# Last pair of expert slots: up product in two column halves, down product with the contraction outermost, one-hot products at the end

## The reference

```python
logits = t @ switch_w + switch_b
route_prob = jax.nn.softmax(logits, axis=-1)
route_prob_max = jnp.max(route_prob, axis=-1)
routes = jnp.argmax(route_prob, axis=-1)
for e in range(n_experts):
    h = jax.nn.gelu(t @ w1[e] + b1[e])      # 1024 -> 512
    y = h @ w2[e] + b2[e]                   # 512 -> 1024
    out = jnp.where((routes == e)[:, None], y, out)
out = out * route_prob_max[:, None]
```

## Time and profile before

| | us |
|---|---|
| median of 3 runs | 586.93 (584.77 to 587.86) |
| profiled execution | 584.88 |
| its span, first to last instruction | 583.2 |
| TensorE matmul busy | 554.5 (95%) |
| VectorE busy | 381.9 (65%) |
| ScalarE busy | 240.0 (41%) |
| up product of the last pair begins | 552.92 |
| last row add on VectorE ends | 578.20 |

### The profile page before, as it was taken

The page is one execution under the profiler, slowest core; times in us unless marked ns, Lnnn a source line. Parts: engine busy times, 40 slices in busy tenths (PEclk is TensorE's granted clock), DMA queues, the critical chain, the costliest instruction groups (busy, mean ns, idle before and its releaser), DMA issues.

```text
span 583.2 us, 8532 instructions
## 1 busy us (share of the span) xinstructions
PE 554.5 (95%) x3054; PEld 473.9 (81%) x3054; DVE 381.9 (65%) x747; ACT 240.0 (41%) x390; POOL 148.4 (25%) x161
## 2 busy tenths in 40 slices
PE   3989999999999999999999999999998998999985
PEld 3989997897999999999979999999997886633321
DVE  6688887865777346773548888888889886200114
ACT  3646554320243333353427556756576513320000
POOL 5627666851176500081000001001002010000020
PEclk9999999999999999999999999999998997999999
DMA  8655557530263554438523125416349688199943
GB/s 304 215 141 184 176 167 248 143 112 1 63 180 128 170 196 137 142 119 287 162 82 132 58 90 123 128 58 160 132 156 326 225 311 338 62 383 412 411 174 112
DMA packets 33778, 104.19 MB, mean 179 GB/s; under 512 B 5424, under 2 KB 9712, under 8 KB 33744
## 3 DMA queue, kind: packets, MB, share of 16 engines
q1 hardware_dynamic: 28224, 89.95, 44.6%
q0 software_dynamic: 5376, 13.29, 8.6%
q10 hardware_dynamic: 144, 0.52, 0.3%
HBM read 96.58 MB, written 5.60 MB: 175 GB/s over the span
## 4 chain that ended last, share of the span: by engine, by line
PE 80%; DVE 11%; ACT 4%; issue 3%; DMA 1%; POOL 0%; DVEq 0%; SPq 0%; ACTq 0%
PE ps L1604 41%; PE ps L1955 10%; PE ps L1797 6%; PE ps L1618 5%; DVE wsp L954 4%; PE ps L1901 2%; PE ps L1741 2%; PE ps L1751 2%; PE ps L1726 2%; PE ps L1688 2%; PE ps L1669 2%; PE ps L1761 2%; ACT wsp L660 1%; DMA tok<-in_x 1%; DVE big L954 1%
## 5 line engine op out<-in xcount | busy, mean ns | idle before, releaser
L1604 PE MATMUL ps<-big,wsp 128*128 128x384 f32 x1656 | 295.7, 336 | 3.2 <-DVE wsp L954 2.7
L1604 PEld LDWEIGHTS ps<-big,wsp 128*128 128x128 f32 x1656 | 286.0, 188 | 7.8 <-issue 5.3
L954 DVE TENSOR_TENSOR wsp<-raw,wsp 128x1024 fp32r<-128x1024 f32 x85 | 110.5, 1304 | 30.4 <-ACT wsp L660 29.5
L660 ACT ACTIVATE wsp<-raw 128x1024 fp32r<-128x1024 f32 x83 | 86.9, 1052 | 32.9 <-PE ps L1618 12.9
L569 POOL DMA_INDIRECT edge_table<-ef,eidx x48 | 56.0, 1167 | 33.0 <-DMA edge_table<-ef,eidx 19.2
L667 ACT ACTIVATE big<-ps,bias 128x384 f32 x24 | 14.0, 583 | 80.8 <-PE ps L1604 80.8
L1955 PE MATMUL ps<-blocks 128*64 128x512 f32 x192 | 43.8, 599 | 0.0
L965 DVE SCALAR_TENSOR_TENSOR big<-ps,bias,big 128x384 f32 (+1 forms) x24 | 14.8, 617 | 34.2 <-ACT big L667 33.5
L784 ACT ACTIVATE work<-work,snm 128x384 f32<-128x384 f32 x48 | 28.9, 604 | 16.1 <-DVE snm L1221 16.1
L1618 PE MATMUL ps<-wsp,big 128*128 128x512 f32 x144 | 33.2, 390 | 0.3 <-DVE wsp L954 0.3
L1618 PEld LDWEIGHTS ps<-wsp,big 128*128 128x128 f32 x144 | 26.9, 188 | 6.3 <-DVE wsp L954 0.8
(11 more groups left out here) (249 smaller groups left out, 715.3 us busy)
## 6 DMA issues: line engine op xcount, KB each, us to landing
raw<-in_w_stream SPq DMA_DIRECT2D x85, 512.0 KB, 4.1
blocks<-in_w_experts SPq DMA_DIRECT2D x64, 512.0 KB, 9.1
rowbuf<-in_rowb POOLq DMA_DIRECT2D x6, 512.0 KB, 6.6
raw_x<-in_w_stream SPq DMA_DIRECT2D x4, 512.0 KB, 6.3
slot_y<-rowbuf POOLq DMA_DIRECT2D x7, 256.0 KB, 5.7
tok<-in_x SPq DMA_DIRECT2D x3, 512.0 KB, 4.0
edges_a<-in_src_rows SPq DMA_DIRECT2D x8, 192.0 KB
edges_a<-in_dst_rows SPq DMA_DIRECT2D x8, 192.0 KB
```

The lines of the kernel that those rows point to most:

```text
L660: nc.scalar.activation(wsp[:, 0, slot, :], raw[:, slot, :], ACT.Copy).then_inc(w_hi, 1)
L954: return nc.vector.tensor_tensor(dst, value, hi.bitcast(F32), ALU.subtract)
L1604: ins = nc.tensor.matmul(ps[:, bank, 0:N], wsp[:, a, slot, k * P:(k + 1) * P], moving[:, b, k, :], start=(k == 0 and n == 0), stop=(k == K ...
```

## The change

Three edits, all in the last pair. (a) The up product is computed as columns 0 to 255 for all eight contraction steps, then columns 256 to 511, each half in its own PSUM bank with its own bias product; all eight blocks are waited for at the start. ScalarE's copy and Gelu and TensorE's transposes work on halves, and the transposes of half 0 stand in the middle of the second half of the up product, those of half 1 behind the first quarter of the down product. (b) The down product first does contraction steps 0 and 1 for both halves of the columns, then steps 2 and 3 for both; both bias products stand ahead. The blocks are loaded in that order. (c) Both groups of one-hot products stand at the end, and VectorE copies y half 0 after the first two gathered row adds and not ahead of them.

```diff
+DOWN_ORDER = ((0, 1, 2, 3),) * (TWOS - 1) + ((0, 2, 1, 3),)
 def down_blocks(p):
-    return [s * QE + RING + j for j in range(RING) for s in (2 * p, 2 * p + 1)]
+    return [s * QE + RING + j for j in DOWN_ORDER[p] for s in (2 * p, 2 * p + 1)]
...
+            def copy_up_half(half):
+                if half == 0:
+                    act.wait_ge(u_half, 1)
+                else:
+                    act.wait_ge(blk_read, read_after("up", TWOS - 1))
+                nc.scalar.activation(u_buf[:, half * 2 * P:(half + 1) * 2 * P], ps[:, 1 - half, 0:2 * P], ACT.Copy)\
+                    .then_inc(u_copied, 1)
+            def hidden_half(half):
+                act.wait_ge(ht_ready, TWOS + half)
+                nc.scalar.activation(h_buf[(TWOS - 1) % 2][:, half * 2 * P:(half + 1) * 2 * P],
+                                     ps[:, 2 + half, 0:2 * P], ACT.Gelu_apprx_tanh).then_inc(ht_act, 1)
...
-            for p in range(TWOS):
+            for p in range(TWOS - 1):
                 copy_up(p)
                 hidden(p)
+            for half in range(2):
+                copy_up_half(half)
+            for half in range(2):
+                hidden_half(half)
...
-                dve.wait_ge(blk_read, read_after("down", p, 2 * h + 2))
+                dve.wait_ge(blk_read, read_after("down", p, 2 * h + 2 if p < TWOS - 1 else h + 3))
...
-            y_rows(TWOS - 1, 0)
             for t in range(2):
                 rows_added(t, 1, mixed)
-            dve.wait_ge(mixed, 2)
-            perm_rows_added(0, 0, 2)
-            y_rows(TWOS - 1, 1)
+            for h in range(2):
+                y_rows(TWOS - 1, h)
             rows_added(2, 1, mixed)
             dve.wait_ge(mixed, NT)
-            perm_rows_added(0, 2, NT)
-            perm_rows_added(1, 0, NT)
+            for h in range(2):
+                perm_rows_added(h, 0, NT)
...
+            def last_up(p):
+                rows = [two_blocks() for j in range(RING)]
+                for half in range(2):
+                    cols = slice(half * 2 * P, (half + 1) * 2 * P)
+                    nc.tensor.matmul(ps[:, 1 - half, 0:2 * P], two_hot(p), b12r[:, cols], start=True, stop=False)
+                    for k in range(KT):
+                        if (half, k) == (1, KT // 2):
+                            hidden_half(p, 0)
+                        for s in range(2):
+                            first = k % 2 * HALF + half * 2 * P
+                            ins = nc.tensor.matmul(ps[s * SLOT:(s + 1) * SLOT, 1 - half, 0:2 * P],
+                                                   slot_x(k, 2 * p + s), rows[k // 2][s][:, first:first + 2 * P],
+                                                   start=False, stop=(k == KT - 1))
+                            if half and k % 2:
+                                ins.then_inc(blk_read, 1)
+                    if half == 0:
+                        ins.then_inc(u_half, 1)
+            def hidden_half(p, half):
+                pe.wait_ge(u_copied, p + 1 + half)
+                for i in range(2):
+                    k = 2 * half + i
+                    ins = nc.tensor.transpose(ps[:, 2 + half, i * P:(i + 1) * P], u_buf[:, k * P:(k + 1) * P], ident)
+                ins.then_inc(ht_ready, 1)
+            def last_down(p):
+                pe.wait_ge(y_sum, 2 * (p - 1))
+                for h in range(2):
+                    nc.tensor.matmul(ps[:, y_bank(p, h), :], two_hot(p), b12r[:, F + h * HALF:F + (h + 1) * HALF],
+                                     start=True, stop=False)
+                for j in range(2):
+                    for h in range(2):
+                        if h == 0:
+                            pe.wait_ge(ht_act, p + 1 + j)
+                        products(y_bank(p, h), lambda k, s: h_buf[p % 2][:, k * P + s * SLOT:k * P + (s + 1) * SLOT],
+                                 (2 * j, 2 * j + 1), j == 1)
+                        if (j, h) == (0, 0):
+                            hidden_half(p, 1)
...
-            up(TWOS - 1)
-            hidden(TWOS - 1)
+            last_up(TWOS - 1)
+            last_down(TWOS - 1)
             pe.wait_ge(perm_set, 1)
-            down(TWOS - 1, lambda: permuted(0))
-            permuted(1)
+            for h in range(2):
+                permuted(h)
```

More of the change, by code:

```diff
@@ L320, in graph_layer @@
         x2t_half = sem("x2t_half")
+        u_half = sem("u_half")
         swt_set, l_ready, l_copied = sem("swt_set"), sem("l_ready"), sem("l_copied")
@@ L935, in _ @@
                     nc.scalar.activation(u_buf[0:SLOT, :], ps[0:SLOT, 0, :], ACT.Copy).then_inc(u_copied, 1)
-                    act.wait_ge(ht_ready, TWOS + o + 1)
+                    act.wait_ge(ht_ready, TWOS + 1 + o + 1)
                     of_slot = [a.rearrange("p (k n) -> p k n", n=P)[:, :, 0:SLOT] for a in (h_buf[0], ps[:, 2, :])]
@@ L2041, in _ @@
                     late_product(o, 0, b12r[:, 0:F], lambda k: x_late[:, k, :], 0, RING)
-                    pe.wait_ge(u_copied, TWOS + o + 1)
+                    pe.wait_ge(u_copied, TWOS + 1 + o + 1)
                     for k in range(F // P):
@@ L2046, in _ @@
                     ins.then_inc(ht_ready, 1)
-                    pe.wait_ge(ht_act, TWOS + o + 1)
+                    pe.wait_ge(ht_act, TWOS + 1 + o + 1)
                     if o:
```

## The result

| | us |
|---|---|
| before, 20 runs timed beside it | 585.66 (583.96 to 587.86) |
| changed, 20 runs | 583.40 (580.98 to 585.87) |
| ratio | 0.996, 95% interval 0.9949 to 0.9972 |
| span of the profiled execution | 581.6 (before 583.2) |

The change wins 2.3 us, 0.4%.

The account below looks back on a forecast made before the run. TensorE's chain, a 2.06 us serial wait on ScalarE and VectorE's queued end bound the kernel; VectorE ending 1.98 earlier and the stores bring the span from 583.2 to 580.8, 2.4 off median 586.93: 584.5, range 582.3 to 587.3.

Parts of the forecast that it names:

- The sum as a whole: From the last up product's first bias product to the end of the span: the change saves 2.4 us; chance 0.47.
- TensorE's stages: Last up product through last down product: ends at 569.78 us, where the same work before ended at 570.76.
- the logits' tiles: Last up product: high end for a 256-column pair, 0.254 us, taken from the router logits' 32-wide tiles.
- a constant of a pair: Last up product: each 256-column pair pays 0.026 us beside 0.208 for its columns, so 0.234.
- Rival 3: Last up product: 64-wide tiles' weight loads can't run beside products; 1.9 us slower, median 588.8; chance 0.09.
- What covers the new waits: Last pair: ScalarE's half copies and Gelus all fit beside TensorE's work with 1.2 us to spare, costing nothing.
- One-hot products and row adds: Kernel's end: six products 0.92 us apart, adds running beside them; VectorE ends at 576.22, 1.98 us earlier.
- The stores: After the row adds: instruction fetches hold the fourth store's issue for 1.8 us; the span ends at 580.8.
- rival 1: Final stores: the instruction fetches miss them; gain 2.9 to 4.1 us, median 583.9 to 582.8; chance 0.20.
- rival 2: Last stages: small losses from pairs, closely spaced stores or a late gather add up; gain 1.6 us, median 585.3; chance 0.22.
- over 4.5 us: Kernel's end: sign of being wrong, if the stores take more than this from the last add to the end.
- the store over 1 us: Kernel's end: expected sign that the fourth or fifth store takes over 1 us to issue.

Follow-up runs that it names:

- quarters: Changed kernel with the last up product in four column quarters of 128 instead of two halves of 256; 583.73 us in a single run.
- Gelu first: Changed kernel with ScalarE's order copy 0, Gelu 0, copy 1, Gelu 1 instead of both copies, then both Gelus; 584.67 us in a single run.
- halves only: Kernel before with only the up product in halves and both down biases ahead; ratio 0.9988, 585.16 against 586.18 us.
- contraction outermost undone: Changed kernel with the column halves of the down product outermost again, one-hot products still at the end; ratio 0.9957.
- gathered add first: "Gelu first" plus VectorE's third gathered row add ahead of its copy of the second y half; ratio 0.9946, 582.17 against 585.63 us.
- only the one-hot products: Kernel before with only the one-hot products moved to the end and VectorE's new order; ratio 0.9956, 583.24 against 586.18 us; second timing 0.9975.
- both biases together: "gathered add first" plus both bias products of the last up product at its start; ratio 0.9939, 581.34 against 585.63 us; second timing 0.9949.

## Why the prediction was right, point by point

- **The sum as a whole.** From S to the end of the span 27.9 us was forecast and 27.6 measured. It is near because most terms were, and also because two misses have opposite signs: 0.35 too much up to the last row add beyond TensorE's stages, 0.2 too little in the stores.
- **TensorE's stages.** The sum to the last down product, 16.86, was met at 16.80. The up product was 8.41 for 8.51 predicted. A pair of 256 columns took 0.225 in a row, not 0.234: of the values in the prediction the low end, exact halving, 0.221, was the nearest, and 0.254 from the logits' tiles was far off. The stretches show why: 8 pairs took 1.88 and 16 took 3.60, so 0.215 a pair and 0.16 once; for quarters 16 and 32 pairs took 1.90 and 3.64, so 0.109 a pair and again 0.16 once. What I took for a constant of a pair is paid once a stretch.
- **Rival 3, weight loads in the open.** It did not happen. In the changed kernel a pair takes 0.225 where the loads of one take 0.14, and with quarters 0.114. The Trainium skill's rule (TensorE: Matmul & The Clock Gate, Part 3: Packing small matmuls — row/col tiling), by which the loads would overlap only where row groups differ, disagrees with both numbers: two tiles with the same rows and other columns hide their loads completely, down to 128 columns. One such load took 0.14 us in the traces, where the prediction's estimate from the page was 0.053.
- **What covers the new waits.** One cover was misread. The prediction had Gelu 0 beside the last eight pairs of the up product. ScalarE works in order and both copies stand ahead of both Gelus, so Gelu 0 waited for the end of the up product. It cost 0.08, since the biases covered the rest; "Gelu first" took it away. The cover of Gelu 1, which the contraction outermost makes, is worth 0.46 to TensorE (halves only; contraction outermost undone). The gathered adds ahead of the copy of y half 0 cost nothing, as predicted: the copy began at 569.08, released by TensorE.
- **One-hot products and row adds.** The term was too large by 0.4: 5.76 from the start of the six to the start of the last row add, measured 5.34 (570.77 to 576.11). I had used 0.92 a product, a third of a stretch that ends in a change of tile shape; the results come 0.86 apart, as the row adds of "gathered add first" do, and that makes 0.3 of it. The other 0.1 is the first result: a row add could start 1.05 behind the start of the first product and not 1.16. The last row add itself took 0.75, since 0.68 is the pace of adds that follow each other. The mechanism was right: the last row add is released by TensorE, and the copy, the gathered add and the first adds run beside the products. But VectorE had 0.1 us of room where the prediction had 0.4. "Gathered add first" gives it more room, and the last row add ends at 22.70 as in "Gelu first", so it is TensorE that sets the end. This part is the larger part of the gain, as "only the one-hot products" shows: of 2.39 us up to the last row add it makes 1.51.
- **The stores.** Here the prediction was lucky: the size was near by two errors that cancel. I had the fourth store held for 1.8 us and the last landing in 3.3. What happened, SyncE's second store, the fetch from 573 to 574 us and the landing of the last:

```profile
574.21 0.58 SPq L494 DMA_DIRECT2D out_dram<-tok  x1
```

```profile
q8 instruction: 1, 0.02, 6.0%
```

```profile
out_dram<-tok SPq DMA_DIRECT2D x1, 256.0 KB, 4.2
```

The second store took 0.58 and no other was held, which is rival 1; but the six stores came 0.66 apart and the last landed only after 4.2 us, which is rival 2. Tail: 4.8 for 4.6 predicted. The prediction had named over 4.5 us as a sign of being wrong, below its own sum of 4.6, and by that sign, and by the store over 1 us that did not come, its account of the stores was wrong. (Rival 1's upper median, 583.9, should be 586.93 - 2.9 = 584.0; nothing rests on it.) Whether the spacing alone makes the landing long is open: "gathered add first" (stores further apart, tail 4.2) speaks for it, but a second fetch of 1.4 us also began at 577.00, beside the last store.

Here is the third store of "both biases together" in its two executions, the longest of the new ones:

```profile
571.90 1.48 SPq L494 DMA_DIRECT2D out_dram<-tok  x1
```

```profile
572.49 1.52 SPq L494 DMA_DIRECT2D out_dram<-tok  x1
```

I had laid the fetch to TensorE's jump at the end of its list and put it behind the last products. That misread the kernel before already: its first fetch began at 576.07, and its one-hot products ran until 577.14. In the traces the fetch starts a nearly fixed time after VectorE's copy of the second y half begins, whatever stands between on VectorE, and the longer it takes the longer a store is held:

| | copy starts | fetch starts, takes | longest store issue | last row add to end of span |
|---|---|---|---|---|
| before | 573.55 | 576.07, 2.02 (a second: 576.35, 1.49) | 1.80 | 5.0 |
| halves only | 574.43 | 577.18, 0.96 | 0.68 | 4.8 |
| one-hot at the end only | 570.22 | 572.88, 1.34 | 0.97 | 5.2 |
| changed | 570.80 | 573.45, 0.96 | 0.58 | 4.8 |
| changed, second execution | 569.58 | 572.22, 1.24 | 0.85 | 4.9 |
| Gelu first | 571.80 | 574.43, 1.31 | 0.92 | 5.1 |
| gathered add first | 569.79 | 572.43, 1.32 | 0.86 | 4.2 |
| both biases together | 568.42 | 571.15, 1.87 | 1.48 | 5.2 |
| both biases together, second execution | 569.01 | 571.74, 1.91 | 1.52 | 4.8 |

In every kernel but the one before, the held store's issue ends 0.36 to 0.39 us after the fetch does, which is about the length of an undisturbed issue: it is as if the store waited for the fetch to end. A store issued up to 0.22 us after the fetch's start was not held; the next one was. The fetch's length differs between two executions of one kernel (0.96 and 1.24), and with six stores 0.66 apart the tail tends to be longer with a longer fetch, 4.8 to 5.2; what makes a fetch long was not found.

The distance from the copy to the fetch is 2.5 to 2.75 us in all of them. That copy is the last thing that TensorE's list waits for, so this fits a TensorE whose sequencer, once released, runs ahead of its products to the end of the list. Counted from the end of the last down product the distance is 2.5 to 2.9, hardly less regular. That it is TensorE's fetch was not tried and stays open.

## What to carry to other kernels

When one engine holds the chain nearly everywhere, look at what queues behind its last product: moving work that nobody else could start on to the very end, so that the other engine's queue drains beside it, won more here (1.51 us up to the last row add) than closing a 2 us wait by splitting (0.34 alone, 0.88 once the split's own new wait was covered too). Before splitting a product to hide a copy, look for small independent products that fit into the wait; two bias products did here what the halves did. And price a split by its changes of tile shape and its extra setup, not by a constant for each product.

## What the runs showed of the hardware

- On two 64-column tiles of the array, a pair of 4-byte product records costs 0.442 us for 512 columns, 0.225 for 256 and 0.114 for 128: nearly proportional to the columns, with weight loads of 0.14 us fully hidden. The prediction had 0.234 to 0.254 for 256 columns.
- A lone full-width product between 64-wide ones costs about 0.2 us more than one that follows another of its shape (0.32 against 0.11 at 256 columns).
- With an instruction fetch of 16 KB under way that takes 0.96 to 2.0 us, the issue of a store takes 0.58 to 1.80 us, 0.2 to 0.5 less than the fetch, where an undisturbed one takes 0.33 to 0.43. Its end follows the end of the fetch by 0.36 to 0.39 us in all kernels but the one before.
- The time at which a profiled execution reaches a given stage, with the same work up to it, scatters by 3 us (552.05 to 555.16 for S), in part through short drops of the granted clock that fall at other places (near 35, 135 or 444 us) and differ in number; the stages from S to the last row add repeat to 0.01 us.
